# First layer of a two-layer transformer: the softmax exponentials read the score banks directly, one head at a time

## The reference

```python
q = (query @ Wq + bq).reshape(B, Sq, H, D)          # H = 16 heads of D = 32
k = (key @ Wk + bk).reshape(B, Sk, H, D)            # Sk = 77
v = (value @ Wv + bv).reshape(B, Sk, H, D)
scores = jnp.einsum('bqhd,bkhd->bhqk', q, k) * scale
scores = jnp.where(mask, jnp.float32(-1000000000.0), scores)
probs = jax.nn.softmax(scores, axis=-1)
ctx = jnp.einsum('bhqk,bkhd->bqhd', probs, v).reshape(B, Sq, H * D)
return ctx @ Wo + bo
```

## Time and profile before

| what | value |
|---|---|
| median of three runs | 2924.67 us (2924.58 to 2933.68) |
| profiled execution, its own time | 2921.61 us |
| its span, first to last instruction | 2919.8 us |
| busy over the span: TensorE, VectorE, ScalarE, GpSimd | 91%, 69%, 52%, 52% |
| mean granted TensorE clock | 0.953 of full speed |
| attention steps of the first layer | about 79 to 605 us of the span |
| exponentials of line 756 | 32, 39.2 us busy |
| shifts of line 876 | 128, 0.478 us each (median) |

### The profile page before, as it was taken

One profiled execution on the slowest core, in us unless ns is written; L12 is line 12 of the kernel. 1 busy time (PEld: TensorE's weight loads), 2 busy tenths in 40 slices (PEclk: granted clock), 3 DMA queues, 4 the chain that ended last, 5 costly groups with the idle time before them and its releaser, 6 DMA issues. The chain is left out here.

```text
span 2919.8 us, 41005 instructions
## 1 busy us (share of the span) xinstructions
PE 2646.1 (91%) x14566; PEld 2188.7 (75%) x14566; DVE 2023.6 (69%) x4005; ACT 1517.6 (52%) x2897; POOL 1522.0 (52%) x1149
## 2 busy tenths in 40 slices
PE   6699999986778699999999999999999998799698
PEld 5577777763436588888888888888888887677476
DVE  3677777742546377777777777777777777577666
ACT  2234334331213277777777777777777777111175
POOL 2355544320000166666666666666666666465555
PEclk9899999998878899999999999999999999899899
DMA  5212222133348633334333343233433314668475
GB/s 188 56 54 56 56 57 57 41 96 128 139 145 312 228 74 80 106 83 115 81 77 109 80 118 81 75 111 76 122 80 77 109 51 136 210 238 288 157 275 187
DMA packets 212526, 351.15 MB, mean 120 GB/s; under 512 B 75839, under 2 KB 82370, under 8 KB 204631
## 3 DMA queue, kind: packets, MB, share of 16 engines
q1 hardware_dynamic: 193539, 284.89, 32.8%
q0 software_dynamic: 11680, 45.02, 4.2%
q10 hardware_dynamic: 7104, 18.61, 1.6%
HBM read 172.47 MB, written 156.64 MB: 113 GB/s over the span
## 5 line engine op out<-in xcount | busy, mean ns | idle before, releaser
L1880 POOL TENSOR_SCALAR pa_Pr<-pa_Pr,pa_rs 128x590 f32<-128x590 f32 x512 | 902.4, 1769 | 485.1 <-DVE pa_rs L2109 484.9
L2113 DVE TENSOR_REDUCE pa_least<-pa_S 128x1 f32<-128x590 f32 x512 | 390.7, 763 | 230.0 <-PE pa_S L1944 227.9
L2034 ACT ACTIVATE pa_Pr<-pa_S,pa_least 128x590 f32<-128x590 f32 x512 | 385.5, 753 | 99.4 <-DVE pa_least L2113 96.0
L2066 DVE TENSOR_TENSOR pa_PTl<-pa_W,pa_PTh 128x512 fp32r<-128x512 f32 (+1 forms) x640 | 421.2, 684 | 20.5 <-ACT pa_PTh L2005 16.4
L2005 ACT ACTIVATE pa_PTh<-pa_W 128x512 fp32r<-128x512 f32 (+1 forms) x640 | 367.0, 596 | 58.4 <-PE pa_W L1955 47.1
L1955 PE MATMUL pa_W<-pa_ident,pa_Pr 128*128 128x128 f32 (+1 forms) x2560 | 369.7, 275 | 0.6
L1955 PEld LDWEIGHTS pa_W<-pa_ident,pa_Pr 128*128 128x128 f32 (+1 forms) x2560 | 302.4, 142 | 30.0 <-POOL pa_Pr L1880 2.8
L1971 PE MATMUL pa_O<-pa_PTh,pa_V 128*128 128x512 f32 (+1 forms) x640 | 289.2, 452 | 18.6 <-DVE pa_PTl L2066 14.4
L1972 PE MATMUL pa_O<-pa_PTl,pa_V 128*128 128x512 f32 (+1 forms) x640 | 253.4, 396 | 0.0
L1942 PE MATMUL pa_S<-pa_U,pa_Qh 128*128 128x296 f32 (+1 forms) x1024 | 228.9, 305 | 7.5 <-ACT pa_Pr L2034 0.5
L1942 PEld LDWEIGHTS pa_S<-pa_U,pa_Qh 128*128 128x128 f32 x1024 | 183.2, 188 | 55.5 <-ACT pa_Pr L2034 21.3
(11 more groups left out here) (503 smaller groups left out, 6545.6 us busy)
## 6 DMA issues: line engine op xcount, KB each, us to landing
xs_s<-pa_Ql SPq DMA_DIRECT2D x57, 576.0 KB
pa_Um<-pa_U SPq DMA_DIRECT2D x128, 147.5 KB
pa_Qh<-pa_Qh SPq DMA_DIRECT2D x128, 128.0 KB
o_s<-pa_O_hi SPq DMA_DIRECT2D x64, 256.0 KB, 2.0
o_s<-pa_O_lo SPq DMA_DIRECT2D x64, 256.0 KB, 2.3
Wkv_hi<-o_s SPq DMA_DIRECT2D x8, 2048.0 KB, 11.3
Wkv_lo<-o_s SPq DMA_DIRECT2D x8, 2048.0 KB, 17.0
l_xa<-x SPq DMA_DIRECT2D x8, 1024.0 KB, 6.5
```

Of the source, the lines that this page charges most:

```text
L1880: pool.tensor_scalar(p, p, rs[:, g % 2, t:t + 1], None, ALU.mult).then_inc(*pool_s.mark("probs", n))
L2034: act.activation(Pr[g % 2][:, t, :], scored[n % 2], ACT.Exp, scale=-1.0, bias=least[:, g % 2, t:t + 1], accum_out=rs[:, g % 2, t:t + 1]).t ...
L2066: dve.tensor_tensor(out, src, f32(hi_ap), ALU.subtract).then_inc(*dve_s.mark(*name))
L2113: dve.tensor_reduce(least[:, g % 2, t:t + 1], scored[n % 2], AX, ALU.min).then_inc(*dve_s.mark("least", n))
```

## The change

ScalarE now takes the exponentials from the score bank itself. VectorE's `shift` no longer touches the scores: it multiplies the four maxima of a tile by `-SCALE`, a 128x4 operation in place. ScalarE then runs one activation per head, Exp of `SCALE * score + bias` with the head's scaled maximum as bias column, four a tile, from PSUM to the buffer `E`, and the last of the four frees the bank. The 1232-column exponential is gone. In ScalarE's order the four groups of step `s + 1` stand at four places: before the output copy, between the two probability copies, after them, and where the one exponential stood. The row sum waits for the last group.

```diff
-        reader = {"S": dve_s, "Q": dve_s, "PT": dve_s, "O": dve_s, "xT": dve_s, "fT": dve_s, "Wo": dve_s, "h": act_s,
+        reader = {"S": act_s, "Q": dve_s, "PT": dve_s, "O": dve_s, "xT": dve_s, "fT": dve_s, "Wo": dve_s, "h": act_s,
...
+            def exponentials(s, t):
+                act.wait_ge(*dve_s.after("shift", s, t))
+                for h in range(HC):
+                    m = act.activation(E[s % 2][:, t, h, :], tile(s, t)[:, h, :], ACT.Exp, scale=SCALE, bias=mx[s % 2][:, t, h:h + 1])
+                m.then_inc(*act_s.mark("free", "S", s, t))
+
             for s in steps:
                 b, c = divmod(s, C)
+                if group(s + 1):
+                    exponentials(s + 1, 0)
...
                 if group(s):
                     probabilities_hi(s, 0)
+                if group(s + 1):
+                    exponentials(s + 1, 1)
+                if group(s):
                     probabilities_hi(s, 1)
+                if group(s + 1):
+                    exponentials(s + 1, 2)
...
                 if group(s + 1):
-                    e = (s + 1) % 2
-                    act.wait_ge(*dve_s.after("free", "S", s + 1, NT - 1))
-                    act.activation(both[:, e, :], both[:, e, :], ACT.Exp, scale=SCALE).then_inc(*act_s.mark("exp", s + 1))
+                    exponentials(s + 1, NT - 1)
...
             def shift(s, t):
                 dve.wait_ge(*dve_s.after("max", s, t))
-                dve.tensor_tensor(E[s % 2][:, t, :, :], tile(s, t), mx[s % 2][:, t, :].unsqueeze(2).to_broadcast([P, HC, SK]),
-                                  ALU.subtract).then_inc(*dve_s.mark("free", "S", s, t))
+                dve.tensor_scalar(mx[s % 2][:, t, :], mx[s % 2][:, t, :], -SCALE, None, ALU.mult).then_inc(*dve_s.mark("shift", s, t))
...
-                    dve.wait_ge(*act_s.after("exp", s + 1))
+                    dve.wait_ge(*act_s.after("free", "S", s + 1, NT - 1))
```

More of the change, by code:

```diff
@@ L364, in claim, with tile @@
             return bank[n]
+        def tile(s, t):
+            return bank_of["S", s, t][:, 0:HC * SKP].rearrange("p (h s) -> p h s", h=HC)[:, :, 0:SK]
         block = ctx.enter_context(nc.Block())
@@ L865, in read_out_lo @@
                 lo_of(oT[1][:, s % OS, :], bank_of["O", s][:, :], oT[0][:, s % OS, :], "O", s, bias=bv[:, d:d + 1])
-            def tile(s, t):
-                return bank_of["S", s, t][:, 0:HC * SKP].rearrange("p (h s) -> p h s", h=HC)[:, :, 0:SK]
             def maximum(s, t):
```

## The result

The changed kernel takes 2989.3 us (median of four runs, 2979.1 to 2992.4) against 2929.2 for the kernel before in the same runs: a ratio of 1.0202 (1.0176 to 1.0229), which is 59 us. The forecast was 2974, in a range of 2944 to 2993. The profiled execution took 2986.74 us, 65.1 more than the one of before.

A forecast was written before the change was run, and what follows sets the result against it. TensorE was taken to set the pace, waiting for score banks and ScalarE's line 748. Terms 22.2 + 8.5 + 3.9 + 4.6 + 3.4 + 4.2 + 3.3 = 50.1 us on 2921.61, plus 3.1 for the median, gave 2974; range 2944 to 2993.

The forecast's parts named there:

- The slot copy: ScalarE's copy of slot sums out of bank 6 (line 748, c = 3 steps): queries start 4.4 us later, five places, 22.2 us.
- The clock behind it: After each of the five longer slot-copy waits TensorE runs at the lower clock: 1.7 us each, 8.5 us, or nothing.
- the late bank of the fourth tile: In c = 3 steps, the delay of TensorE's fourth score tile was taken to lie inside the slot-copy wait already counted.
- c = 2: Third step of a batch: score banks free 0.65 us later in seven places, 4.6 us, plus 3.4 us of lower clock, or nothing.
- c = 0: First step of a batch: the table load now precedes the first exponentials, fourth tile 0.7 us later in six places, 4.2 us.
- c = 1: Second step of a batch: the bank term, score banks free 0.65 us later in six places, 3.9 us.
- The first batch: First four steps, where TensorE waits for the last block of probabilities: 3.3 us together, between nothing and 7.2.
- The price of an exponential: On ScalarE, one of 128x77 takes 0.32 us, the next starts 0.22 us later; a tile of four ends after 0.98 us.
- VectorE did not set the pace: Denies the rival that VectorE sets the pace, so banks come free sooner and the change is faster: 2912 us, chance 6%.
- the second rival: The slot copy is not the wait that grows, as ScalarE reaches it as early as before: 2944 us, chance 8%.
- the rival of longer chains: Exponentials do not overlap and longer chains reach the second probability block's read-out: 70 us and more, 2995 or above, 6%.
- the two signs of being wrong: Queries in c = 3 start under 2 us after the fourth score tile, or TensorE's layer waits grow under 25 us.

## Why the prediction was right

By the profiled executions the change costs 65.1 us where the sum had 50.1. Of the 15 us between them 6.6 lie up to the last scored step and 8.5 behind it, where the prediction had nothing: 5.7 at the end of the layer and 2.8 behind it, within the spread of that rest.

**The slot copy, 22.2 us, right in kind, too small.** The walk said that the queries start 4.4 us later in the step. Measured from the step's first score tile they start 9.95 us after it (350.17 to 360.12) instead of 4.16 (333.71 to 337.87): 5.8 later. The missing 1.4 us are the two scalings, 0.93 and 0.80 where the sum had 0.15 each. With the maxima in PSUM they start 8.54 us after it (349.62 to 358.16), 4.38 later, which is the walk's number. The term that was mis-sized is the price of the scaling, taken from a 128x1 row that had no GpSimd work beside it. That the copy is the cause, and not a place where another loss shows, is settled by the kernel with the slot copy first.

The Trainium skill ("SBUF — State Buffer", Who interferes with whom) has this: a `tensor_scalar` can enter a mode that takes VectorE's second port pair, which GpSimd shares. Whoever issues first gets the pair for its whole instruction, and the other is blocked. The runs agree: all 32 long scalings of the changed kernel began behind a GpSimd operation that was still running, 0.93 us for the one beside its additions, and with PSUM as the source none took over 0.165 us. That not every scaling that met GpSimd was long, as said above, stays open.

**The clock behind it, 5 x 1.7 us.** The query product took 4.82 us against 2.90, 1.9 a step, at a granted clock of 0.56. With the 5.8 that is 7.7, and the c = 3 steps took 7.3 to 7.7 more: 37.4 in all where the two terms had 30.7. That difference of 6.7 us is about what the steps' sum (56.7) lies above the forecast (50.1). The other terms balance in sum, which is partly luck, as two of them below show. The prediction said that the late bank of the fourth tile lies inside the wait already counted; it showed as a wait of its own (0.66 us), but belongs to the same chain.

**c = 2: as forecast, 6.5 us in five steps.** The forecast's 4.6 and 3.4 were for seven steps, 6.7 for these five. Three steps grew by 0.67 to 0.69, and the two whose waits of about 1.8 us passed 2.4 grew by 2.2, with the lower clock behind them.

**c = 0: 4.2 forecast, 4.5 measured,** and shown to be the table load by taking it away.

**c = 1: 3.9 forecast, 4.5 measured, and the agreement is luck.** In none of the six does a bank wait show; the first tiles of the step shown above ran mostly at the lower level (0.57), and so TensorE reached the bank when it was free. The mean clock over each of the six steps was 0.89 to 0.91. Before it was 1.00 in four of them and 0.90 in two; those four grew by 1.0 to 1.2 us and the two by nothing. So the 4.5 us are the lower clock, which the sum did not have for these steps. The bank term itself was well sized where the clock stayed up: in the kernel with the slot copy first the same step kept its clock (1.00), and the wait of 0.16 us grew by 0.70, where 0.65 was forecast:

```profile
377.89 0.38 PE L119 MATMUL l_bank<-l_Kd_hi,l_qT_hi 128*128 128x312 f32 x1 [0.86 <-ACT l_E L729]
```

Why the clock was low at the head of these steps, with TensorE busy ahead of it, is not settled.

**The first batch: 3.3 forecast, 3.7 measured** in the first nine steps, and this agreement shows little. The wait that the term was built on, for the last probabilities, grew only from 7.7 to 8.7 us. And two kernels whose edits do not reach these steps, the kernel before with its slot copy first and the same with the router later, differ there from the kernel before by +2.6 and -1.2 us. What the change costs there stays open.

**The price of an exponential** held: four took 0.97 us (0.98 forecast). The estimate from the ScalarE page of the Trainium skill ("ScalarE: Activation LUTs", What ACT_TABLE_LOAD costs) was 1.10; the trace is nearer to the row of line 1220.

**The rivals.** VectorE did not set the pace: its busy time in the 22 steps fell from 279.5 to 263.9 us and the steps took longer. But the sentence that its routing follows TensorE's own products, so that nothing brings it forward, was wrong. The router's steps stood ahead of the maximum by order and not by need, and moving them gave 5.7 us in the c = 2 steps over the kernel with its slot copy first. The slot copy is the wait that grew most, against the second rival. And no read-out waited: TensorE's waits in the 22 steps are the two kinds shown above and 1.5 us for other low parts, as before, so the rival of longer chains is out too. Of the two signs of being wrong neither came: the queries in c = 3 start 6.4 us after the fourth score tile (353.69 to 360.12), and the waits for slot copy and score banks grew by 32 us together.

## What to carry to other kernels

Before an operation is put into an engine's queue, list what stands behind it there and who waits for that: an engine that is idle more than half of the time can still be late at the one copy that a bank hangs on, and moving that copy gave back 34 of 59 us. Move work onto an engine only at places where it waited anyway, and look whether a small new operation is held up by a neighbour that is busy just then (0.93 us for 0.16 here). Where a step seems bound by an engine's lateness, ask whether what stands ahead in its queue must be there: moving 1.4 us of routing took 5.7 us out of the five c = 2 steps.

## What the runs showed of the hardware

- A 128x4 multiplication from SBUF to SBUF on VectorE took 0.16 to 0.17 us alone and up to 0.93 us in the changed kernel where it began beside a running GpSimd operation (32 of 69 over 0.25 us); with PSUM as the source none of 69 that met GpSimd took more than 0.165 us.
- A bias column costs an exponential of 128x77 from PSUM 68 ns (334 against 266 ns), and a group of four 0.35 us (0.97 against 0.62), since the next one starts later too.
- The same 367 matmuls with nearly the same idle time took 88 us at a granted clock of 0.92 and 93 at 0.87: at the end of the layer an earlier start of 5 us was lost again.
